# A vision block with a mixture of experts on one core: where the zero fill runs, when weights are loaded, and how the last expert's rows end

## The reference

```
# 64 images of 96x96x3; 36 patches of 768 values each, plus a class token: 64 x 37 = 2368 rows of 256
z = layernorm(patches) * g1 + b1;  z = layernorm(z @ W_proj + b_proj) * g2 + b2     # 768 -> 256
h = concat(cls, z) + pos_emb
n = layernorm(h);  q, k, v = n @ Wq + bq, n @ Wk + bk, n @ Wv + bv
h = h + softmax(mask_diagonal(q / 256 @ k.T)) @ v                                   # per image
x = layernorm(h);  top 2 of 8 experts per row by softmax(x @ router_w + router_b), weights normed
each expert keeps its 444 rows of highest weight:
    out[row] += weight * (gelu(x[row] @ w1[e] + b1[e]) @ w2[e] + b2[e])             # 256 -> 1024 -> 256
h = h + layernorm(out) * ln_g + ln_b
```

## Time and profile before

| | us |
|---|---|
| median of 3 runs (lowest, highest) | 460.95 (460.77, 461.57) |
| the profiled execution: its time / its span | 460.41 / 458.7 |
| attention stage (first transfer to last logits), about | 0 to 198 |
| routing, about | 198 to 248 |
| experts, first gather to last project, about | 248 to 435.6 |
| end, about | 435.6 to 458.7 |
| busy: TensorE, VectorE, ScalarE, GpSimd | 357.1, 317.6, 250.4, 239.5 |

### The profile page before, as it was taken

How to read it: one execution, slowest core, us unless ns; L and a number is a source line. 1 busy time by engine, 2 the same in 40 slices (tenths; PEclk the granted TensorE clock), 3 DMA queues, 4 the chain that set the end, 5 groups by cost and what they waited for, 6 DMA issues and landing times.

```text
span 458.7 us, 8052 instructions
## 1 busy us (share of the span) xinstructions
PE 357.1 (78%) x2212; PEld 316.3 (69%) x2212; DVE 317.6 (69%) x853; ACT 250.4 (55%) x526; POOL 239.5 (52%) x434
## 2 busy tenths in 40 slices
PE   3799539999999999650017299999999999999900
PEld 1598429999989997440007089999999999999700
DVE  7657237788778765869888035688787877878660
ACT  4356326777877775343000056777877686677400
POOL 3257426777878776400003740046776868655462
PEclk9899959999999999765555579999999999999965
DMA  6641321554454233478201953355868667562211
GB/s 179 180 111 47 101 70 51 151 133 128 144 139 140 74 96 103 134 218 88 1 0 29 256 137 120 108 154 166 252 182 237 197 189 235 160 174 59 72 40 40
DMA packets 49265, 58.40 MB, mean 127 GB/s; under 512 B 12153, under 2 KB 37993, under 8 KB 49230
## 3 DMA queue, kind: packets, MB, share of 16 engines
q1 hardware_dynamic: 42588, 43.11, 34.2%
q0 software_dynamic: 5568, 14.09, 11.2%
q10 hardware_dynamic: 1074, 0.79, 0.6%
HBM read 36.74 MB, written 21.36 MB: 127 GB/s over the span
## 4 chain that ended last, share of the span: by engine, by line
PE 68%; DVE 10%; POOL 5%; DMA 5%; issue 3%; SPq 3%; ACT 3%; POOLq 0%; DVEq 0%; ACTq 0%
PE pz L869 18%; PE pall L882 17%; PE pall L765 8%; DVE wproj L1142 5%; PE pall L715 5%; PE pall L722 4%; DMA stage<-in_x 3%; PE pz L695 2%; PE pall L740 2%; PE pall L748 2%; SPq L398 2%; PE pall L731 2%; DMA held<-x_rows,gidx 2%; PE pall L775 1%; PE pall L894 1%
## 5 line engine op out<-in xcount | busy, mean ns | idle before, releaser
L869 PE MATMUL pz<-halves 128*128 128x448 f32 x384 | 90.9, 373 | 2.1 <-DVE halves L1234 2.1
L882 PE MATMUL pall<-halves 128*128 128x448 f32 x384 | 90.1, 370 | 0.8 <-DVE halves L1229 0.8
L869 PEld LDWEIGHTS pz<-halves 128*128 128x128 f32 x384 | 73.7, 192 | 9.1 <-DVE halves L1234 2.5
L882 PEld LDWEIGHTS pall<-halves 128*128 128x128 f32 x384 | 71.0, 188 | 7.2 <-DVE halves L1229 1.1
L646 ACT ACTIVATE wproj<-pz,b1t 128x448 f32<-128x448 f32 x64 | 40.7, 636 | 47.6 <-PE pz L869 47.6
L1229 DVE TENSOR_TENSOR halves<-wproj,halves 128x448 fp32r<-128x448 f32 x64 | 40.2, 628 | 36.4 <-ACT halves L658 36.1
L1451 POOL DMA_INDIRECT held<-x_rows,gidx x32 | 33.0, 1031 | 61.7 <-DVE gidx L1210 52.2
L1476 POOL DMA_INDIRECT out<-rows,didx x32 | 41.4, 1293 | 31.7 <-DVE rows L1272 26.2
L765 PE MATMUL pall<-halves 128*112 128x256 f32 x396 | 53.2, 289 | 3.4 <-DVE halves L973 3.4
L1360 POOL TENSOR_TENSOR rs<-rs,neghalf 112x1 f32<-112x1 f32 x88 | 50.2, 570 | 7.3
L765 PEld LDWEIGHTS pall<-halves 128*112 128x112 f32 x396 | 48.9, 180 | 3.8 <-DVE zbias L992 2.4
(11 more groups left out here) (231 smaller groups left out, 741.2 us busy)
## 6 DMA issues: line engine op xcount, KB each, us to landing
stage<-in_w SPq DMA_DIRECT2D x32, 512.0 KB, 5.0
stage<-in_x SPq DMA_DIRECT2D x64, 108.0 KB
x_rows<-x SPq DMA_DIRECT2D x22, 224.0 KB, 3.0
x_rows<-held SPq DMA_DIRECT2D x22, 224.0 KB, 3.7
sums<-rows SPq DMA_DIRECT2D x7, 448.0 KB, 3.5
out<-held SPq DMA_DIRECT2D x21, 111.0 KB
x_rows<-zero SPq DMA_DIRECT2D x1, 1474.9 KB
wproj<-in_w_proj ACTq DMA_DIRECT2D x1, 768.0 KB
```

Source lines behind the costliest of these rows:

```text
L869: m = nc.tensor.matmul(bank(k % 2)[:, 0:SLOTS], w[:, c, k * 128:(k + 1) * 128], xs[:, e % 2, c, :], start=(n == 0), stop=(n == 3 * EC - 1))
L882: m = nc.tensor.matmul(pall[:, 2 * (e % 2) + o, 0:SLOTS], w[:, k, o * 128:(o + 1) * 128], hs[:, k % 2, :], start=(k == 0 and n == 0), stop ...
```

## The change

1. **x2 slots.** `x2` has four slots instead of two, each with its own semaphore, so that ScalarE waits for the store of four tiles ago.
2. **Zero fill.** It moves from SyncE's step 2 to its step 18. The rows 112 to 127 of all blocks are written from 16 partitions of zeros, 46 blocks each, instead of from 46 partitions, 16 rows each. The bytes are the same.
3. **First gathers.** SyncE waits for the last gather of expert 0 before it loads expert 1's first weights. VectorE's low halves of expert 0's first weights come after `sidx`, and wait for the second gather.
4. **Last expert.** In expert 7's chunks 5 and 6 VectorE does all four `row_diff` and all four `row_final` of expert 6. VectorE, not ScalarE, adds b2 to the second half of expert 7's output. Its four slots go to four PSUM banks, and each is announced by itself. Its rows are written to a buffer of their own (`lastfin`), so the wait for expert 6's scatters goes. Roots and scatters run in two pairs.

```diff
-        x2 = sb("x2", [P, 2, ED])
+        x2 = sb("x2", [P, 4, ED])
+        lastfin = sb("lastfin", [P, JT, ED])
...
+        def final_of(e):
+            return lastfin if e == E - 1 else fin
+        def rows_bank(e, j):
+            if e < E - 1:
+                return pall[0:P, 4 + j // 2, (j % 2) * ED:(j % 2 + 1) * ED]
+            return (pall[0:P, 4 + j, 0:ED] if j < 2 else pz[0:P, j - 2, 0:ED])
+        def rows_ready(e, j):
+            return 2 * e + (j if e == E - 1 else j // 2) + 1
...
-                if isinstance(i, int) and i == 2:
+                if isinstance(i, int) and i == 18:
...
-                    sp.dma_start(x2_rows.rearrange("(q p) f -> q p f", p=128)[:, P:128, :],
-                                 rep(zero[0:Q + 2, 0:XW].rearrange("q (a f) -> q a f", a=1), 1, 128 - P)).then_inc(s_fill, 16)
+                    sp.dma_start(x2_blocks[P:128, :, :],
+                                 rep(zero[0:128 - P, 0:XW].rearrange("p (a f) -> p a f", a=1), 1, Q + 2)).then_inc(s_fill, 16)
...
+            sp.wait_ge(g_in[0][JT - 1], 16)
             for e in range(1, E):
...
-            y_transposed(E - 1)
+            y_transposed(E - 1, range(1))
...
+            dve.wait_ge(r_list2, 1)
+            V_.tensor_scalar(sidx[:, :], bank(5)[0:P, 0:COLS].bitcast(u32), 16, 64 * 128 - 1, ALU.logical_shift_right,
+                             ALU.bitwise_and).then_inc(r_sidx, 1)
+            dve.wait_ge(g_in[0][1], 16)
             for pr in range(2):
                 w1_low(0, pr)
             for pr in range(2):
                 w2_low(0, pr)
...
-                if j == 0:
+                if j == 0 and e < E - 1:
                     need(dve, o_out, 16 * JT * e)
...
+                    elif k in (5, 6):
+                        for j in range(JT):
+                            (row_diff if k == 5 else row_final)(e - 1, j)
...
+            dve.wait_ge(y_k, E * HC)
+            V_.tensor_scalar(yT[:, 1, :], pall[:, 2 * ((E - 1) % 2) + 1, 0:SLOTS], col(b2t, E * EC - 1), None, ALU.add)\
+                .then_inc(yt_sb, 1)
...
-            for g in range(2):
-                root(E - 1, g)
-            scatter(E - 1)
+            root(E - 1, 0)
+            scatter(E - 1, range(2))
+            root(E - 1, 1)
+            scatter(E - 1, range(2, JT))
```

More of the change, by code:

```diff
@@ L295, in vit_tower @@
         g_rs0 = sem("g_rs0"); g_rs = sem("g_rs"); g_nb = sem("g_nb"); x2_ok = sem("x2_ok")
-        x2_out = [sem("x2_out0"), sem("x2_out1")]
+        x2_out = [sem(f"x2_out{k}") for k in range(4)]
         x2T_ps = sem("x2T_ps"); x2T_sb = sem("x2T_sb"); l_ps = sem("l_ps"); l_sb = sem("l_sb")
@@ L498, in _ @@
             sp.wait_ge(g_col, 64)
-            for par in range(2):
-                sp.wait_ge(x2_out[par], 16 * (TILES // 2))
+            for k in range(4):
+                sp.wait_ge(x2_out[k], 16 * ((TILES - k + 3) // 4))
         @block.scalar
@@ L647, in gelu, with y_transposed @@
                                      bias=col(b1t, u)).then_inc(u_sb, 1)
-            def y_transposed(e):
+            def y_transposed(e, parts=range(EC)):
                 act.wait_ge(y_k, (e + 1) * HC)
                 need(act, y_ps, 2 * e)
-                for o in range(EC):
+                for o in parts:
                     nc.scalar.activation(yT[:, o, :], pall[:, 2 * (e % 2) + o, 0:SLOTS], ACT.Identity,
@@ L1290, in finish_rows @@
                             row_mean(e - 1, j)
-                    if k in (6, 7):
-                        for j in range(2 * k - 12, 2 * k - 10):
-                            row_diff(e - 1, j)
-                    if k == 7:
-                        row_final(e - 1, 0)
+                    if e < E - 1:
+                        if k in (6, 7):
+                            for j in range(2 * k - 12, 2 * k - 10):
+                                row_diff(e - 1, j)
+                        if k == 7:
+                            row_final(e - 1, 0)
+                    elif k in (5, 6):
+                        for j in range(JT):
+                            (row_diff if k == 5 else row_final)(e - 1, j)
             x_low(0)
@@ L1440, in _ @@
             pool.wait_ge(r_idx, 1)
-            for par in range(2):
-                pool.wait_ge(x2_out[par], 16 * (TILES // 2))
+            for k in range(4):
+                pool.wait_ge(x2_out[k], 16 * ((TILES - k + 3) // 4))
             pool.wait_ge(s_fill, 48)
@@ L1468, in root, with scatter @@
                 G.tensor_tensor(frs[:, 1, a:b], frs[:, 0, a:b], rep(neghalf[:, :], 1, b - a), ALU.pow).then_inc(f_rs, 1)
-            def scatter(e):
+            def scatter(e, js=range(JT)):
                 need(pool, o_out, 16 * JT * e)
-                for j in range(JT):
+                for j in js:
                     k = e * JT + j
```

51 lines of the change are left out of this document (23 added, 28 removed).

## The result

The changed kernel takes 445.96 us (median of 4 runs, 444.85 to 446.79), beside 461.02 for the kernel before: a ratio of 0.967 (95% interval 0.964 to 0.970), 15.1 us faster. The forecast was 439.0 with a range up to 443.5. It is outside, by 2.5 us of the range and 7.0 of the forecast. The profiled execution took 445.23 us with a span of 443.4.

A forecast was written before the change was run, and what follows sets the result against it. TensorE was taken to bound the kernel, so only its stands and the end chain cost time. 460.41 - 15.3 - 4.4 - 2.2 = 438.5, put at 439.0 for the median, range 436 to 443.5.

The forecast's parts named there:

- A: Attention stage: moving the fill behind the last image load removes TensorE's wait and low clock, 15.3 us (12.9 to 15.6).
- R3: Late zero fill: it does not spread over engines; the hole goes anyway, price 0 to 3 us, 439 to 442; chance 0.04.
- B: Start of the experts: expert 0's fourth gather lands earlier, gain 4.4 us (2.0 to 5.0), held weights cost 0.
- R2: Start of the experts: gathers don't come earlier or held weights come late; gain 0 to 2, 441.5 to 443.5; chance 0.06.
- C: Last expert: GpSimd is free earlier and the chain of roots and scatters is shorter, 2.2 us (0.6 to 3.4).
- The rivals: Four other outcomes: another engine late (0.10), gathers not earlier (0.06), fill not spreading (0.04), slower than before (0.02).
- R4: TensorE's longer unbroken run: granted clock falls to 1.2 GHz; slower than before, 30 us of it give 469; chance 0.02.

The follow-up runs named there:

- e9: Kernel before with only the zero fill's new shape and new place, x2 still in two slots: 453.6 us (0.986).
- e10: Kernel before with only the zero fill's new shape, in its old place: 444.64 us (0.966).
- e5: Changed kernel with 64 one-column matmuls added to TensorE's program in the routing, on chip W: 438.66 us (0.953).
- e11: e5 with the zero fill's old shape (46 rows) in the new place, on chip X: 449.09 us (0.977).
- e17: The changed kernel itself, run once more on chip Z beside e18: 446.36 us (0.965).
- e18: The kernel of e5, run on chip Z beside e17: 446.09 us (0.9665).
- e2: Kernel before with only the change to the first gathers, on chip V: 462.98 us (1.0029).
- e3: Changed kernel with GpSimd's gathers of experts 2 and 3 held until expert 0's fourth gelu, on chip V: 441.69 us (0.957).
- e4: Changed kernel with 32 one-column copies added to ScalarE's program in the routing, on chip V: 445.09 us (0.9645).
- e7: Changed kernel with SyncE's hold of expert 1's weights lengthened to expert 0's fourth gelu, on chip W: 438.9 us (0.953).
- e8: e3 without SyncE's hold of expert 1's weights, on chip W: 439.73 us (0.954).
- e16: e5 with the zero fill in its new shape put back in the old place, on chip Y: 445.33 us (0.9645).
- e1: Changed kernel with the change to the first gathers undone, on chip V: 444.7 us (0.963).

## Why the prediction was wrong

**A, right in size.** 15.3 was forecast, 15.60 came; TensorE kept the high clock, and nothing else came late. Two sentences beside the sum were wrong. "About 1.5 MB at the 288 GB/s ... is 5 us on the DMA engines": it is 15 us, since these packets move at 98 GB/s with the engines full. I took the rate of weights and gathers for a fill of another form, though the earlier trace rows had a fill's rate on two engines, 49 GB/s, to warn me. And "the x2 slots themselves are worth nothing": with two, the late fill takes 9 us back (e9 453.6, e10 444.64 on the same chip). The price of a narrow late fill, "0 to 3 us", was 11 by the ratios of e5 and e11. None of it changed the sum, as the change has four slots and a wide fill. The stated reason for A, the load behind a fill on two engines, is right, and the shape alone cures it (e10). The place alone cures it too, as R3 said, but then the narrow fill costs 10 us further on (e11).

**B, the step that failed.** The gathers came as forecast: 0.93 for the second issue, 7.47 us from the first issue to the fourth use (7 to 8 said), 4.97 us gained for 4.4. What failed is "1 MB of weights and 2.8 MB of gathers at 288 GB/s take 13 us, to about 269. Cost 0, with little to spare". I asked of this crowd only whether the held weights land in time. They did, and no wait for weights shows, so R2 is not what happened either. I didn't ask what else meets 16 us of gathers when the experts start in their midst. Measured: 4.35 us of a stand and the low clock behind it, 7.00 in all in the changed kernel, and a stand of 4.07 to 4.81 us in every like version on three of five chips. On W the time came as forecast: 438.66 us (e5) for 439.0. e5 differs from the change only by matmuls that e17 and e18 show to be without effect on Z, but the change itself was not run on W or X.

**C, near in size by luck.** 1.71 came for 2.2, but from the wrong one of its two halves. The first half, GpSimd free earlier, was put at 0.6 and gave 1.9: GpSimd began expert 7's root 3.64 us after the last project, beside 5.55 before. The forecast had added 0.4 us to each of three gathers of sums for the VectorE instructions moved beside them. They took 1.11, 1.14, 0.94 and 0.93, and before the change 1.11, 0.94, 1.13 and 0.93, so the move slowed them by nothing. The Trainium skill's rule (GPSIMD Engine Reference, Key points), which spoke against part C, shows no such cost here: the two gathers beside the four `row_final` took 0.94 and 0.93. The second half, roots and scatters in pairs, was put at 1.8 less 0.2 and gave nothing: from the start of that root to the last scatter's end it takes 9.96 us, beside 9.76 before. After each root the first scatter starts 1.49 and 1.47 us later, where I had counted 0.65 and 0.45, one `row_final` and (the first time) the landing. The second of them follows its own `row_final` by 0.9 us, a hand-over for which I had no term; the first starts as late after its own, with the landing of expert 6's last scatter (issued 3.7 us before it) due about then. That 1.3 us more here and 1.8 less there nearly cancel is chance.

**The rivals.** None of the four happened. R4 had the right fear in the wrong place: TensorE's granted clock fell while it stood (to 0.50 at about 255.3, 2 us into the stand), and in the unbroken run of the attention stage it is high in every slice from the 3rd to the 15th (22 to 166 us).

**What is shown, and what is not.** Shown: part B's gain is handed back in expert 0 on some chips (e2, e17); taking the later gathers out of the experts' start removes that (e3, 441.69 beside 445.09 for e4 on the same chip); the shift of an engine's program does not (e4, e18). Not settled is what connects TensorE's signals to the gathers, and why chips, or sittings, differ. e3 removed all crowding there, so it doesn't tell GpSimd's issues from the gathers' transfers, nor these from the weights; e7 and e8, made for this, ran on a chip without the stand.

## What to carry to other kernels

When a change lets the compute start earlier beside a fixed stream of transfers, look at what that stream now overlaps, and push the part of it that isn't urgent behind the start: e3's one wait was worth 3.4 us against e4 on chip V, where the stand occurs, and on chip W, e8, which has it too, was at 0.954 beside 0.953 for e5, no loss that is clear of the noise. Before believing that a small edit cured a stall, run the uncured kernel beside it on the same chip: e17 and e18 did at once what the runs from e4 to e16 had not done. For a slow fill, first change its shape: e10's two lines brought the whole 15.5 us that A gave with a new place and two more buffers.

## What the runs showed of the hardware that was not expected

- The same kernel took 438.66 us on one chip and 446.09 on another (1.7%), while the kernel before took 461.2 and 461.75 there. Nearly all of it is one stand of 4.8 us and the clock behind it (experts 172.04 and 178.33 us). Whether it is the chip or the sitting, no run tells.
- TensorE's granted clock fell to 0.50 within the stand of 4.35 us and came back 6.8 us later, at 262.2; in e1's stand of 2.19 us it did not fall.
- A fill of 1.5 MB from 16 partitions kept 16 engines at a share of 0.9 for 15 us at 98 GB/s; on two engines 47 GB/s were moved (e11).
- A single DMA issue on SyncE took 20.96 us before and 24.78 in e11 behind a narrow fill, and 3 to 5 us behind a wide one.
